# Routed experts in tiles of two 128-slot halves, each with its own expert

## The chip, the cores and the metric

The kernel runs on one NeuronCore of one Trainium2 chip. Five engines work side by side, each from its own instruction stream, and meet only at semaphores: TensorE (PE), VectorE (DVE), ScalarE (ACT), GpSimd (POOL) and SyncE (SP), whose queue issues most DMAs. The metric is the device time of one execution in microseconds. The kernel before takes 455.58 us, the median of three runs (455.02 to 456.61).

## The reference, cut to what matters

A block with gated cross attention and a gated mixture of experts, for 32 sequences of 128 tokens of width 128 (T = 4096 tokens):

```python
x = x + tanh(g_xattn[0]) * attention(layernorm(x), ctx)     # 16 heads of 8
xf = layernorm(x).reshape(4096, 128)
# two shared experts, of which the mean is taken
sh = gelu(einsum('td,sdh->sth', xf, sW1) + sb1)              # hidden 512
shared = (einsum('sth,shd->std', sh, sW2) + sb2).mean(axis=0)
# eight routed experts, two for each token
gates = xf @ rW + rb
topk_vals, topk_idx = top_k(gates, 2)
w = softmax(topk_vals) scattered to the chosen experts
h = gelu(einsum('td,edh->eth', xf, W1) + b1)
moe = einsum('te,etd->td', w, einsum('eth,ehd->etd', h, W2) + b2)
x = x + tanh(g_ffn[0]) * (shared + moe)
```

Each row of `xf` is normalised without a learnt scale, so its 128 values sum to zero.

## The kernel before, in words

The program runs in four stages that follow one another on one core.

**Attention** goes through 16 pairs of sequences, in turns (`turns`, t = 0 to 19) in which each engine does its share of several pairs at once. Queries and keys are split by POOL into two fp16 parts, written by SP to DRAM and read back in another layout. Beside this, the 40 half pieces of expert weights (`SPLITS`) are loaded into staging memory by SP (`load_weights`), measured, scaled and split into fp16 high and low parts by POOL (`split_weights`, from turn 6 on, as many in a turn as `SPLIT_IN` says). Every product with expert weights is then three fp16 matmuls: high times high, low times high, high times low.

**Shared experts** take 16 units (8 groups of 512 tokens by two experts). Beside them DVE picks two experts for each token, counts them, gives each choice a slot, and POOL scatters the normalised rows (with their destination index) into the DRAM list `xs`, sorted by expert. Each expert's slots are padded to a multiple of `TILE` = 256, so the list never holds more than `NTILE` = 39 tiles, and 39 are always run. `tilee` holds the expert of each tile.

**Routed experts** run tile by tile. For tile i: SP loads 256 rows (`XR`); PE transposes them (`row_transposes`, L1122), ACT copies the result (`routed_copy`, L820); PE multiplies with W1 in `routed_up` (L1132), four chunks of 128 hidden values by 256 slots; ACT applies bias and gelu chunk by chunk (`routed_gelu`, L828); DVE splits the result into fp16 high (L1561) and low (L1563) parts, two chunks at a time; PE multiplies with W2 in `routed_down` (L1144), 24 matmuls of 128 by 128; DVE scales and adds the second bias (L1571); POOL scatters two times 128 rows to the DRAM tensor `yd` (L650). PE's order within a step of the loop is up of tile i+1, transposes of tile i+3, down of tile i.

Which weights a tile multiplies with is known only at run time. `TileExperts.load` (L384) therefore reads `tilee` into registers of the engine's sequencer, `LOADS` = 3 tiles at a time, on PE, ACT and DVE, all within the last seven shared units. An address such as `bass.ds(e * HID + c * P, P)` is then worked out by register instructions in front of the matmul that uses it: a fused one for a chunk's first address, a plain one for each further address (FUSED_REGOPS and ALU_OP in the trace, ISA and REGISTER_ALU in the order of the program).

**The tail** reads `yd` back, weighs both choices of each token, adds them to the residual and stores the output.

The bias b1 reaches gelu as a per-partition column (`b1T`), picked by a register for routed tiles; the gates' bias rb is added by DVE.

## Time and profile before

| | |
|---|---|
| median of three runs | 455.58 us |
| the profiled execution | 454.94 us, span 453.1 us (1.8 us lie around the span) |
| mean granted TensorE clock | 0.977 of full speed |
| busy share of the span | PE 85%, DVE 85%, ACT 75%, POOL 68% |
| POOL time in the routed scatters (L650) | 86.8 us, 78 instructions |

Times within the kernel are microseconds from the start of the span. Attention lies at about 15 to 220 us, the shared experts reach to about 317 us, the routed experts to 432 us and the tail to 453 us. A stage's share of busy time tells little where several engines are near full; the chain of waits tells which of them ends last. Matmuls are pipelined on PE: a matmul of 128 columns is listed with 0.22 us, while the next one starts 0.06 us later, so the distance of starts is what counts. [...]

### The profile page before, as it was taken

The numbers are of one execution on the slowest core, as the hardware profiler recorded it, in microseconds if no ns is written. First come the engines' busy times: TensorE is split into PE (matmuls) and PEld (weight loads), VectorE is DVE, ScalarE is ACT, GpSimd is POOL, SyncE is SP. The second block draws the span as 40 slices with busy tenths as digits, with TensorE's granted clock in tenths as the row PEclk, the third lists the DMA queues.
The fourth block names the chain that finished last, engine by engine and source line by source line (L and its number), as shares of the span: only waits on it lengthen the run. The fifth ranks groups of instructions, "written<-read, shape, count | busy, mean of one in ns | idle before, by whom it ended". The sixth has DMA issues, their size and how long they took to land.

```text
span 453.1 us, 14622 instructions
## 1 busy us (share of the span) xinstructions
PE 386.3 (85%) x5155; PEld 316.6 (70%) x5155; DVE 384.9 (85%) x947; ACT 340.8 (75%) x677; POOL 309.7 (68%) x431
## 2 busy tenths in 40 slices
PE   0558889997999899988789999998999999999910
PEld 0335677786788788766557776777899999999900
DVE  7696668978876987899778999887799999999986
ACT  0635677787888788878789986775888888888844
POOL 6252222799899899978777767774177777777740
PEclk9999999999999999999899999999999999999975
DMA  7968884354333334474221111112223333355229
GB/s 192 314 196 214 206 186 110 90 138 98 92 92 98 87 95 107 101 229 175 92 66 49 55 37 53 49 48 69 70 83 96 97 90 93 94 156 158 69 78 294
DMA packets 71686, 53.43 MB, mean 118 GB/s; under 512 B 7209, under 2 KB 63476, under 8 KB 71616
## 3 DMA queue, kind: packets, MB, share of 16 engines
q1 hardware_dynamic: 64896, 43.15, 35.9%
q0 software_dynamic: 4544, 8.44, 5.6%
q10 hardware_dynamic: 2176, 0.91, 0.8%
q8 instruction: 44, 0.72, 0.7%
q14 instruction: 26, 0.21, 0.2%
HBM read 29.51 MB, written 24.33 MB: 119 GB/s over the span
## 4 chain that ended last, share of the span: by engine, by line
POOL 23%; PE 21%; DVE 20%; issue 13%; DMA 10%; SPq 6%; ACT 4%; POOLq 0%; DVEq 0%; ACTq 0%
POOL yd L650 9%; DVE HH L1533 5%; PE pAtt L1144 4%; DMA scr<-QKS 4%; PE pAtt L1090 2%; PE pS L1132 2%; PE pE L1132 2%; DVE t_MX L1257 2%; POOL t_STG L558 2%; POOL t_W2l L562 2%; POOL QKS L548 2%; PE pAtt L928 1%; DMA t_STG<-in_W 1%; POOL xs L628 1%; POOL t_XF L572 1%
## 5 line engine op out<-in xcount | busy, mean ns | idle before, releaser
L650 POOL DMA_INDIRECT yd<-Y,XR x78 | 86.8, 1113 | 37.6 <-issue 23.2
L1257 DVE TENSOR_REDUCE t_MX<-pS 128x4 f32<-128x512 f32 x128 | 86.8, 682 | 22.6 <-PE pS L889 20.0
L748 ACT ACTIVATE PT<-pE,t_mbias,t_scl 128x512 f32<-128x512 f32 x128 | 96.9, 789 | 2.7 <-PE pE L889 2.7
L628 POOL DMA_INDIRECT xs<-t_STG,t_pos x64 | 66.2, 1034 | 23.1 <-issue 14.3
L1563 DVE SCALAR_TENSOR_TENSOR HR<-GG,t_sc,HR 128x512 f16<-128x512 f32 x78 | 58.6, 751 | 2.8
L1144 PE MATMUL pAtt<-t_W2h,HR 128*128 x624 | 59.2, 219 | 0.7 <-DVE HR L1563 0.7
L889 PE MATMUL pS<-t_K,t_Q 128*128 128x128 f16 x512 | 52.0, 228 | 8.5 <-DVE t_MX L1257 5.1
L1144 PE MATMUL pAtt<-t_W2l,HR 128*128 x312 | 54.4, 219 | 0.0
L828 ACT ACTIVATE GG<-pS,t_b1T,t_inv 128x256 f32<-128x256 f32 x78 | 39.8, 561 | 16.9 <-PE pS L1132 16.9
L889 PE MATMUL pE<-t_Q,t_K 128*128 128x128 f16 x512 | 49.9, 220 | 1.6 <-DMA t_Q<-MPl 0.6
L1144 PEld LDWEIGHTS pAtt<-t_W2h,HR 128*128 128x128 f16 x624 | 49.6, 98 | 1.1 <-issue 0.9
L1090 PE MATMUL pAtt<-t_W2h,HH 128*128 128x128 f16 x512 | 46.4, 219 | 1.2 <-DVE HH L1533 1.0
L889 PEld LDWEIGHTS pS<-t_K,t_Q 128*128 128x128 f16 x512 | 35.1, 102 | 13.3 <-DVE t_MX L1257 8.0
L1090 PE MATMUL pAtt<-t_W2l,HH 128*128 128x128 f16 x256 | 44.0, 219 | 0.0
L1090 PEld LDWEIGHTS pAtt<-t_W2h,HH 128*128 128x128 f16 x512 | 40.1, 98 | 3.6 <-DVE HH L1533 2.0
L928 PE MATMUL pAtt<-PT,t_V 128*32 128x128 f32 x1024 | 42.0, 282 | 0.0
L889 PEld LDWEIGHTS pE<-t_Q,t_K 128*128 128x128 f16 x512 | 36.8, 98 | 6.9 <-ACT PT L748 3.8
L828 ACT ACTIVATE GG<-pE,t_b1T,t_inv 128x256 f32<-128x256 f32 x78 | 39.8, 567 | 0.0
L1561 DVE TENSOR_SCALAR HR<-GG,t_sc 128x512 f16<-128x512 f32 x78 | 37.8, 485 | 1.9 <-ACT GG L828 1.3
L546 POOL CAST QKS<-QK 128x512 f16<-128x512 f32 x16 | 9.8, 610 | 42.2 <-ACT QK L666 42.2
L1132 PE MATMUL pE<-XE,t_W1h 128*128 128x256 f16 x156 | 32.1, 273 | 0.0
L1132 PE MATMUL pS<-XE,t_W1h 128*128 128x256 f16 x156 | 31.9, 273 | 0.0
(280 smaller groups left out, 1042.7 us busy)
## 6 DMA issues: line engine op xcount, KB each, us to landing
xs<-t_padrow SPq DMA_DIRECT2D x10, 516.0 KB, 5.1
XR<-xs SPq DMA_DIRECT2D x39, 129.0 KB, 2.3
scr<-QKS SPq DMA_DIRECT2D x16, 256.0 KB, 2.4
t_Q<-scr SPq DMA_DIRECT2D x16, 256.0 KB
t_K<-scr SPq DMA_DIRECT2D x32, 128.0 KB
t_STG<-in_W SPq DMA_DIRECT2D x7, 512.0 KB, 6.6
YY<-yd SPq DMA_DIRECT2D x14, 256.0 KB, 4.2
t_X<-in_x SPq DMA_DIRECT2D x4, 512.0 KB, 7.7
```

What stands on the lines that cost most here:

```text
L628: g.indirect_dma_start(k.xs, bass.IndirectOffsetOnAxis(ap=pos[:, n:n + 1], axis=0), k.PAY[:, n, :], None).then_inc(h.di[q], 16)
L650: g.indirect_dma_start(k.yd, bass.IndirectOffsetOnAxis(ap=XR[u][:, q, D:ROW], axis=0), Y[u][:, q, :], None, bounds_check=2 * T - 1, oob_is ...
L748: act.activation(PT[:, m % NPT], pE[g % 2][:], ACT.Exp, bias=k.mbias[:, bt:bt + 1], scale=k.scl[:, bt:bt + 1]).then_inc(s.exp, 1)
L828: act.activation(G32[i % 2][:, c, :], pU[c][:, 0:TILE], ACT.Gelu, bias=k.b1T[:, bass.ds(e * NC + c, 1)], scale=k.inv[:, 3:4]).then_inc(r.g ...
L889: ins = pe.matmul(out[:, j, :], ko if transposed else qo, qo if transposed else ko, start=True, stop=True)
L928: ins = pe.matmul(pA[bb][32 * j:32 * j + 32, part // 2, :], k.V[pair % NB][:, 4 * bb + j, part, :], PT[:, m % NPT, j, :], start=(part == 0 ...
L1090: ins = pe.matmul(pA[u][:, q, :], HH[e][:, part, c, q * P:(q + 1) * P], w[:, w0:w0 + P], start=(e == 0 and c == 0 and q == 0 and step == 0 ...
L1132: ins = pe.matmul(pU[c][:, 0:TILE], w[:, bass.ds(e * HID + c * P, P)], XE[i % M][:, part, :], start=(step == 0), stop=(step == 2))
L1144: ins = pe.matmul(pA[i % 2][:, q, :], HR[i % M][:, part, c, q * P:(q + 1) * P], w[:, bass.ds(e * HID + c * P, P)], start=(c == 0 and q == ...
L1257: v.tensor_reduce(out=MX[:, n // G % 2, n % G // 4, m % 2, m // 2::2], in_=pS[n % 2][:], axis=AX_X, op=ALU.max).then_inc(s.max, 1)
L1561: v.tensor_scalar(HR[i % M][:, 0, ch, :], G32[i % 2][:, ch, :], k.sc[:, 2:3], None, ALU.mult).then_inc(r.hi, 1)
L1563: v.scalar_tensor_tensor(out=HR[i % M][:, 1, ch, :], in0=G32[i % 2][:, ch, :], scalar=k.sc[:, 2:3], in1=HR[i % M][:, 0, ch, :], op0=ALU.mu ...
```

## The change

`TILE` becomes 128, so 71 tiles (`NTILE`) are always run instead of 39. Two tiles form a duo of 256 slots, and the loop runs over 36 duos (the last has one half). Rows are loaded, transposed, activated and split for the duo as a whole. The products with weights are made for each half with that half's expert, so the up product has 24 matmuls of 128 slots instead of 12 of 256. The second bias is added for each half on its own.

The bias b1 becomes part of the product: as a row's values sum to zero, the last weight row can be subtracted from the other 127 (`fold_last_row` on POOL, with the last row broadcast to all partitions by `load_last_rows` on SP), the last value of each row is set to 1, and the last weight row is replaced by b1 (`hidden_biases`). The same is done for rb in the gates. Gelu then needs no bias column, and takes two chunks (128 by 512) at once; the high part of the second two chunks is made by ACT (`routed_rounding`) instead of DVE. All W1 pieces are now split ahead of all W2 pieces; the W2 pieces are loaded into the place of the broadcast rows, after the fold. `LOADS` becomes 2, and what the shared units don't load is loaded in the routed loop, one load in a step, on PE and DVE; ACT needs none.

```diff
-TILE = 256
+TILE = 128
 NTILE = (2 * T + E * (TILE - 1)) // TILE
-SLOTS = NTILE * TILE
+DUO = 2 * TILE
+NDUO = -(-NTILE // 2)
+SLOTS = NDUO * DUO
...
-    LOADS = 3
+    LOADS = 2
...
+    FOLDS = {LAG: (0, 1), LAG + 1: (2, 3), LAG + 2: (4,)}
...
+            def load_last_rows(n):
+
+                w = (io.W1, io.sW1)[2 * n >= E]
+                e = 2 * n % E
+                for j in range(2):
+                    sp.dma_start(k.weight_pieces[PIECES + n][:, j * HID:(j + 1) * HID], w[e + j, LASTC, :].partition_broadcast(P)).then_inc(k.s_row[n // 3], 16)
+
+            def hidden_biases():
+
+                sp.wait_ge(s.fold, PIECES)
+                sp.dma_start(k.STG[LASTC:D, 0:E * HID], io.b1.rearrange("(o e) h -> o (e h)", o=1)).then_inc(k.s_b1, 16)
+                sp.dma_start(k.STG[LASTC:D, E * HID:NE * HID], io.sb1.rearrange("(o e) h -> o (e h)", o=1)).then_inc(k.s_b1, 16)
...
-                for n in {1: range(4, 6), 2: range(6, 8), 3: range(8, 10)}.get(t, ()):
-                    load_weights(n)
+                if t == 1:
+                    load_weights(PIECES - 1)
+                for n in {1: (0,), 2: (1, 2), 3: (3, 4)}.get(t, ()):
+                    load_last_rows(n)
+                if t == LAG + 2:
+                    hidden_biases()
+                for n in {LAG + 1: (0, 1), LAG + 2: (2, 3), LAG + 3: (4,)}.get(t, ()):
+                    sp.wait_ge(s.fold, n + 1)
+                    load_weights(PIECES + n)
...
+            def fold_last_row(n):
+
+                if n == 0:
+                    g.wait_ge(s.sq, PIECES)
+                g.wait_ge(k.s_row[n // 3], 16 * 2 * (3, 2)[n // 3])
+                for j in range(2):
+                    piece = k.weight_pieces[n][:, j * HID:(j + 1) * HID]
+                    ins = g.tensor_tensor(piece, piece, k.weight_pieces[PIECES + n][:, j * HID:(j + 1) * HID], ALU.subtract)
+                ins.then_inc(s.fold, 1)
...
+                    g.wait_ge(k.s_b1, 32)
                     tables()
+                for n in FOLDS.get(t, ()):
+                    fold_last_row(n)
...
-            for i in range(NTILE):
+            for i in range(NDUO):
                 u = i % N
                 g.wait_ge(r.y, i + 1)
-                for q in range(2):
+                for q in range(parts_of(i)):
...
-            def routed_gelu(i, e, c):
-                act.wait_ge(r.up, NC * i + c + 1)
-                if c % 2 == 0:
-                    wait(act, r.lo, NC // 2 * (i - 2) + c // 2 + 1)
-                act.activation(G32[i % 2][:, c, :], pU[c][:, 0:TILE], ACT.Gelu, bias=k.b1T[:, bass.ds(e * NC + c, 1)], scale=k.inv[:, 3:4]).then_inc(r.gelu, 1)
+            def routed_gelu(i, half):
+                ch, wide = slice(2 * half, 2 * half + 2), TILE * parts_of(i)
+                act.wait_ge(r.up, 2 * i + half + 1)
+                wait(act, r.lo, 2 * (i - 2) + half + 1)
+                act.activation(G32[i % 2][:, ch, 0:wide], pair_of_chunks(i, half)[:, :, 0:wide], ACT.Gelu, scale=k.inv[:, 3:4]).then_inc(r.gelu, 1)
+
+            def routed_rounding(i):
+                wide = TILE * parts_of(i)
+                act.wait_ge(r.gelu, 2 * i + 2)
+                wait(act, r.dn, i - M + 1)
+                act.activation(HR[i % M][:, 0, 2:4, 0:wide], G32[i % 2][:, 2:4, 0:wide], ACT.Copy, scale=k.sc[:, 2:3]).then_inc(r.hia, 1)
...
                 for c in range(NC):
-                    wait(pe, r.gelu, NC * (i - 1) + c + 1)
-                    for step, (w, part) in enumerate(((k.W1h, 0), (k.W1l, 0), (k.W1h, 1))):
-                        ins = pe.matmul(pU[c][:, 0:TILE], w[:, bass.ds(e * HID + c * P, P)], XE[i % M][:, part, :], start=(step == 0), stop=(step == 2))
-                    ins.then_inc(r.up, 1)
+                    if c % 2 == 0:
+                        wait(pe, r.gelu, 2 * (i - 2) + c // 2 + 1)
+                    out = pair_of_chunks(i, c // 2)[:, c % 2, :]
+                    for q in range(last + 1):
+                        tok = slice(q * TILE, (q + 1) * TILE)
+                        for step, (w, part) in enumerate(((k.W1h, 0), (k.W1l, 0), (k.W1h, 1))):
+                            ins = pe.matmul(out[:, tok], w[:, bass.ds(es[2 * i + q] * HID + c * P, P)], XE[i % M][:, part, tok],
+                                            start=(c % 2 == 0 and q == 0 and step == 0), stop=(c % 2 == 1 and q == last and step == 2),
+                                            skip_group_check=True)
+                    if c % 2:
+                        ins.then_inc(r.up, 1)
...
-                    for q in range(2):
+                    for q in range(parts_of(i)):
                         for step, (w, part) in enumerate(((k.W2h, 0), (k.W2l, 0), (k.W2h, 1))):
-                            ins = pe.matmul(pA[i % 2][:, q, :], HR[i % M][:, part, c, q * P:(q + 1) * P], w[:, bass.ds(e * HID + c * P, P)],
+                            ins = pe.matmul(pA[i % 2][:, q, :], HR[i % M][:, part, c, q * P:(q + 1) * P], w[:, bass.ds(es[2 * i + q] * HID + c * P, P)],
...
-            for i in range(NTILE):
-                if i + 1 < NTILE:
-                    routed_up(i + 1, es[i + 1])
-                if i + 3 < NTILE:
+            for i in range(NDUO):
+                if i + 1 < NDUO:
+                    routed_up(i + 1)
+                tile_experts.load()
+                if i + 3 < NDUO:
                     row_transposes(i + 3)
-                routed_down(i, es[i])
+                routed_down(i)
...
             def routed_split(i):
+                wide = TILE * parts_of(i)
                 for half in range(2):
                     ch = slice(2 * half, 2 * half + 2)
-                    v.wait_ge(r.gelu, NC * i + 2 * half + 2)
-                    wait(v, r.dn, i - M + 1)
...
+                    if half == 0:
+                        v.wait_ge(r.gelu, 2 * i + 1)
+                        wait(v, r.dn, i - M + 1)
...
+                    else:
+                        v.wait_ge(r.hia, i + 1)
...
-                v.scalar_tensor_tensor(out=Y[u][:], in0=pA[i % 2][:, 0:2, :], scalar=k.down[:, 0:1], in1=row.to_broadcast([P, 2, D]),
-                                       op0=ALU.mult, op1=ALU.add).then_inc(r.y, 1)
+                for q in range(parts_of(i)):
+                    ins = v.scalar_tensor_tensor(out=Y[u][:, q, :], in0=pA[i % 2][:, q, :], scalar=k.down[:, 0:1], in1=k.b2[:, bass.ds(es[2 * i + q] * D, D)],
+                                                 op0=ALU.mult, op1=ALU.add)
+                ins.then_inc(r.y, 1)
```

How this stands in the order of the program, at three places. First PE, one chunk of the up product of a routed tile before (L1132: W1h and W1l are the weights' high and low parts, XE the transposed rows, pE the chunk's PSUM bank; ISA and REGISTER_ALU are the register instructions that work out an address):

```order
L1132 ISA [waits x_gelu]
L1132 MATMUL pE<-XE,t_W1h 128x256
L1132 REGISTER_ALU
L1132 MATMUL pE<-XE,t_W1l 128x256
L1132 MATMUL pE<-XE,t_W1h 128x256
```

and one chunk of a duo now (L1186):

```order
L1186 ISA [waits x_gelu]
L1186 MATMUL pE<-XE,t_W1h 128x128
L1186 REGISTER_ALU
L1186 MATMUL pE<-XE,t_W1l 128x128
L1186 MATMUL pE<-XE,t_W1h 128x128
L1186 ISA
L1186 MATMUL pE<-XE,t_W1h 128x128
L1186 REGISTER_ALU
L1186 MATMUL pE<-XE,t_W1l 128x128
L1186 MATMUL pE<-XE,t_W1h 128x128
```

Each 256-wide group of three matmuls with one pair of register instructions has become two 128-wide groups with a pair each.

Second PE, from the end of an up product over the transposes (pMix) into the down product (pAtt), before (L1144):

```order
L1132 MATMUL pE<-XE,t_W1h 128x256
L1122 MATMUL pMix<-t_ident,XR 128x128 [waits x_XE,x_ld4]
L1122 MATMUL pMix<-t_ident,XR 128x128 x3
L1144 REGISTER_ALU [waits x_lo,x_y]
L1144 MATMUL pAtt<-t_W2h,HR 128x128
L1144 REGISTER_ALU
L1144 MATMUL pAtt<-t_W2l,HR 128x128
L1144 MATMUL pAtt<-t_W2h,HR 128x128 x2
L1144 MATMUL pAtt<-t_W2l,HR 128x128
L1144 MATMUL pAtt<-t_W2h,HR 128x128
```

and now (L1201):

```order
L1186 MATMUL pE<-XE,t_W1h 128x128
L394 TENSOR_LOAD tilee
L1171 MATMUL pMix<-t_ident,XR 128x128 [waits x_XE,x_ld3]
L1171 MATMUL pMix<-t_ident,XR 128x128 x3
L1201 REGISTER_ALU [waits x_lo,x_y]
L1201 MATMUL pAtt<-t_W2h,HR 128x128
L1201 REGISTER_ALU
L1201 MATMUL pAtt<-t_W2l,HR 128x128
L1201 MATMUL pAtt<-t_W2h,HR 128x128
L1201 REGISTER_ALU
L1201 MATMUL pAtt<-t_W2h,HR 128x128
L1201 REGISTER_ALU
```

The load of two expert numbers (TENSOR_LOAD, in 22 of the 36 steps) stands between up and transposes, and the down product has two register instructions for every three matmuls where it had two for every six.

Third SP's queue at the end of turn 4 and the start of turn 5 (t_K is the keys' place in SBUF, t_rows the bounds on the weights, scr the DRAM copy of queries and keys), before:

```order
L487 DMA t_Q<-scr 64x8x256
L490 DMA t_K<-scr 32x8x256 x2
L435 DMA t_rows<-kwm 128x384
L467 DMA scr<-QKS 128x2x512
L469 DMA scr<-QKS 128x2x256
```

and now:

```order
L514 DMA t_Q<-scr 64x8x256
L517 DMA t_K<-scr 32x8x256 x2
L439 DMA t_STG<-in_W 128x8x128 x2
L462 DMA t_rows<-kwm 128x384
L494 DMA scr<-QKS 128x2x512
L496 DMA scr<-QKS 128x2x256
```

Two weight loads that stood at the ends of turns 1 and 2 are now issued here, ahead of the load of the bounds and of the next turn's stores.

## Rows read from the trace of the kernel before

**Rows 1.** View by stretch: length, busy of PE, PEld, DVE, ACT, POOL, clock, DMA

```profile
320.00:432.00 112.00, 111.34 (x1540) 104.90 (x1537) 107.53 (x194) 94.00 (x194) 82.87 (x74) 1.00 0.33 96
```

**Rows 2.** Chain of waits, two routed tiles: start us, length us, what ended last

```profile
331.01 1.34 PE pAtt L1144 x24
332.35 0.66 PE pS L1132 x6
333.01 0.66 PE pE L1132 x6
...
333.89 1.34 PE pAtt L1144 x24
```

**Rows 3.** Groups of instructions, 320 to 432 us: count | busy us, mean ns

```profile
L1561 DVE TENSOR_SCALAR HR<-GG,t_sc 128x512 f16<-128x512 f32 x78 | 37.8, 485 | 1.9 <-ACT GG L828 1.3
...
L1563 DVE SCALAR_TENSOR_TENSOR HR<-GG,t_sc,HR 128x512 f16<-128x512 f32 x78 | 58.6, 751 | 2.8
...
L1571 DVE SCALAR_TENSOR_TENSOR Y<-pAtt,t_down,t_b 128x256 f32<-128x256 f32 x38 | 18.1, 478 | 0.0
...
L828 ACT ACTIVATE GG<-pE,t_b1T,t_inv 128x256 f32<-128x256 f32 x78 | 39.8, 567 | 0.0
...
L820 ACT ACTIVATE XE<-pMix 128x512 f16<-128x512 f16 x37 | 22.5, 608 | 0.0
```

**Rows 4.** The same view, ACT in the shared experts, 225 to 317 us

```profile
L795 ACT ACTIVATE HH<-GG,t_sc 128x512 f16<-128x512 f32 x22 | 15.7, 730 | 0.0
...
L803 ACT ACTIVATE GG<-pS,t_b1T,t_inv 128x512 f32<-128x512 f32 x16 | 11.6, 781 | 5.4 <-PE pS L1027 5.4
```

**Rows 5.** Instructions of L1132, 345.6 to 346.6 us; PEldq is PE's sequencer

```profile
L1132 PEldq FUSED_REGOPS  x4: 46/46/46, 345.7 to 346.4; - x4
L1132 PEldq ALU_OP  x4: 32/32/32, 345.8 to 346.5; - x4
...
L1132 PE MATMUL pS<-XE,t_W1h x1: 273/273/273, 346.6 to 346.6; 128*128 128x256 f16 x1
```

**Rows 6.** The same view of L1144, 346.9 to 348.4 us

```profile
L1144 PEldq ALU_OP  x8: 32/32/32, 347.0 to 348.3; - x8
```

**Rows 7.** Instructions of PE in order of time, first routed tile

```profile
320.82 0.28 PE L1132 MATMUL pE<-XE,t_W1h 128*128 128x256 f16 x1
320.94 0.27 PE L1132 MATMUL pE<-XE,t_W1l 128*128 128x256 f16 x1
...
321.99 0.22 PE L1144 MATMUL pAtt<-t_W2h,HR 128*128 x1
322.10 0.22 PE L1144 MATMUL pAtt<-t_W2l,HR 128*128 x1
```

**Rows 8.** Instructions that read tilee: duration min/median/max ns, first and last start

```profile
L384 PEldq TENSOR_LOAD <-tilee x13: 762/794/963, 281.8 to 314.4; - x13
```

**Rows 9.** Instructions of POOL in order of time, turn 4

```profile
59.03 0.61 POOL L546 CAST QKS<-QK 128x512 f16<-128x512 f32 x1 [5.60 <-ACT QK L666]
59.72 1.16 POOL L548 TENSOR_TENSOR QKS<-QK,QKS 128x512 f16<-128x512 f32 x1
```

**Rows 10.** Instructions of SP's queue in order of time, end of turn 4

```profile
70.50 0.45 SPq L435 DMA_DIRECT2D t_rows<-kwm  x1
72.25 0.38 SPq L467 DMA_DIRECT2D scr<-QKS  x1
```

**Rows 11.** Chain of waits, after the last tile

```profile
434.88 0.87 POOL yd L650
...
436.17 3.12 DMA yd<-Y,XR
```

**Rows 12.** View by stretch, around the one dip of the clock in mid-kernel

```profile
219.00:220.00 1.00, 0.08 (x1) 0.11 (x1) 0.93 (x4) 0.00 (x0) 0.92 (x2) 1.00 0.07 19
221.00:222.00 1.00, 0.98 (x10) 0.55 (x12) 0.90 (x5) 1.00 (x4) 0.85 (x3) 0.50 0.00 0
```

**Rows 13.** Groups of instructions of PE inside that dip, 221 to 224 us

```profile
L889 PE MATMUL pE<-t_Q,t_K 128*128 128x128 f16 x4 | 0.6, 308 | 0.0
```

More of the change, by code:

```diff
@@ L241, in layer @@
     SPLIT = LAG + 3
-    FIRST_W2 = 12
-    SPLITS = [(which, e, half) for which, e in ((0, 8), (0, 9), (0, 0), (0, 4), (0, 1), (0, 5), (1, 0), (1, 1), (1, 2), (1, 3), (0, 2), (0, 6), (1, 4),
-                                                (0, 3), (0, 7), (1, 5), (1, 8), (1, 9), (1, 6), (1, 7)) for half in range(2)]
+    FIRST_W2 = 2 * NE
+    SPLITS = [(which, e, half) for which, e in ((0, 8), (0, 9), (0, 0), (0, 4), (0, 1), (0, 5), (0, 2), (0, 6), (0, 3), (0, 7),
+                                                (1, 0), (1, 1), (1, 2), (1, 3), (1, 4), (1, 5), (1, 8), (1, 9), (1, 6), (1, 7)) for half in range(2)]
     UNITS = len(SPLITS)
@@ L280, in layer @@
     XR = [lt(f"XR{u}", [P, 2, ROW], I32) for u in range(N)]
-    XE = [lt(f"XE{u}", [P, 2, TILE], F16) for u in range(M)]
-    GG = lt("GG", [P, 2, NC, TILE])
+    XE = [lt(f"XE{u}", [P, 2, DUO], F16) for u in range(M)]
+    GG = lt("GG", [P, 2, NC, DUO])
     G32 = [GG[:, u] for u in range(2)]
     HS = [GG[:].rearrange("p u c t -> p (u c t)").rearrange("p (c t) -> p c t", c=NC), H32[:]]
-    HR = [lt(f"HR{u}", [P, 2, NC, TILE], F16) for u in range(M)]
+    HR = [lt(f"HR{u}", [P, 2, NC, DUO], F16) for u in range(M)]
     Y = [lt(f"Y{u}", [P, 2, D]) for u in range(N)]
@@ L367, in load_results, with parts_of @@
         eng.dma_start(YY[:, j, R * n:R * n + R, :], yv[:, j, R * n:R * n + R, :]).then_inc(f.ld[j][n], 16)
+    def parts_of(i):
+        return min(2, NTILE - 2 * i)
     def all_scattered(eng):
         for u in range(N):
-            eng.wait_ge(r.st[u], 32 * len(range(u, NTILE, N)))
+            eng.wait_ge(r.st[u], 16 * sum(parts_of(i) for i in range(u, NDUO, N)))
     class TileExperts:
@@ L801, in shared_body @@
                     wait(act, h.lo, NC * (i - 2) + c + 1)
-                    col = (E + i % 2) * NC + c
-                    act.activation(HS[i % 2][:, c, :], pU[c], ACT.Gelu, bias=k.b1T[:, col:col + 1], scale=k.inv[:, 3:4]).then_inc(h.gelu, 1)
+                    act.activation(HS[i % 2][:, c, :], pU[c], ACT.Gelu, scale=k.inv[:, 3:4]).then_inc(h.gelu, 1)
                     if c - 1 in on_scalar(i):
                         rounding(i, c - 1)
-                    if c % 2 and i >= LOADING:
-                        tile_experts.load()
                     if i == 3 and c == 0:
@@ L876, in _ @@
             pe.transpose(pA[0][:, 1, 0:B], k.maskf[:], k.identf[0:B, 0:B]).then_inc(s.mr, 1)
-            pe.wait_ge(s.md, 1)
+            pe.wait_ge(s.mb, 2)
             pe.matmul(pA[1][:, 0, 0:5], k.ones[0:5, :], k.mxd[:], start=True, stop=True)
-            pe.matmul(pA[1][:, 1, 0:B], k.ones[:], k.maskT[:], start=True, stop=True).then_inc(s.ma, 1)
+            pe.matmul(pA[1][:, 1, 0:B], k.ones[:], k.maskT[:], start=True, stop=True).then_inc(s.mr, 1)
             pe.wait_ge(k.s_rest, k.rest_in)
-            pe.transpose(b1_cols, k.b1r[:], k.identf[0:NE * NC, 0:NE * NC])
             pe.wait_ge(s.bvr, 1)
@@ L1152, in _ @@
             row_transposes(1)
-            routed_up(0, es[0])
+            routed_up(0)
             row_transposes(2)
-            for i in range(NTILE):
-                if i + 1 < NTILE:
-                    routed_up(i + 1, es[i + 1])
-                if i + 3 < NTILE:
+            for i in range(NDUO):
+                if i + 1 < NDUO:
+                    routed_up(i + 1)
+                tile_experts.load()
+                if i + 3 < NDUO:
                     row_transposes(i + 3)
-                routed_down(i, es[i])
+                routed_down(i)
         @block.vector
@@ L1569, in routed_result @@
                 wait(v, r.st[u], 32 * (i // N))
-                row = k.b2[:, bass.ds(e * D, D)].rearrange("p (o d) -> p o d", o=1)
-                v.scalar_tensor_tensor(out=Y[u][:], in0=pA[i % 2][:, 0:2, :], scalar=k.down[:, 0:1], in1=row.to_broadcast([P, 2, D]),
-                                       op0=ALU.mult, op1=ALU.add).then_inc(r.y, 1)
+                for q in range(parts_of(i)):
+                    ins = v.scalar_tensor_tensor(out=Y[u][:, q, :], in0=pA[i % 2][:, q, :], scalar=k.down[:, 0:1], in1=k.b2[:, bass.ds(es[2 * i + q] * D, D)],
+                                                 op0=ALU.mult, op1=ALU.add)
+                ins.then_inc(r.y, 1)
             es = tile_experts.of
             routed_split(0)
-            for i in range(NTILE):
-                if i + 1 < NTILE:
+            for i in range(NDUO):
+                if i + 1 < NDUO:
                     routed_split(i + 1)
-                routed_result(i, es[i])
+                tile_experts.load()
+                routed_result(i)
             weights_of_choices()
@@ L1625, in program @@
         k.s_c, k.s_x = ([outer.enter_context(nc.semaphore(f"{n}{c}")) for c in range(NT // CHUNK)] for n in ("c_ctx", "c_x"))
-        k.s_one, k.s_pad, k.s_padk, k.s_b2, k.s_rest = (outer.enter_context(nc.semaphore("c_" + n)) for n in ("one", "pad", "padk", "b2", "rest"))
+        k.s_one, k.s_pad, k.s_padk, k.s_b2, k.s_rest, k.s_b1 = (outer.enter_context(nc.semaphore("c_" + n)) for n in ("one", "pad", "padk", "b2", "rest", "b1"))
+        k.s_row = [outer.enter_context(nc.semaphore(f"w_row{n}")) for n in range(2)]
         k.keep = outer
```

88 lines of the change are left out of this document (48 added, 40 removed).

## The prediction

> **What bounds the kernel now.** I read the view by stretch first, to see which stage the change touches and who is full there. In the routed stage, 320 to 432 us, PE is busy 111.34 of 112 us and DVE 107.53, at full clock [rows 1]: two engines are nearly level, so neither can be named from shares. The chain of waits decides: it runs on PE alone, tile after tile, with 1.34 us for the 24 matmuls of a down product, twice 0.66 us for an up product, and 2.88 us from one down product to the next [rows 2]; what is left, 2.88 - 1.34 - 1.32 = 0.22 us, are the four transposes. 39 tiles by 2.88 are the 112 us. DVE, by the groups of instructions, has twice 0.485 and 0.751 and once 0.478 us, 2.95 us with overlaps in it [rows 3], so it comes close behind.
>
> The third view is the one that matters here: the instructions that PE's sequencer handles itself. While the array is in the middle of the down product, the sequencer already works on the next tile's up product: its four fused and four plain register instructions lie between 345.7 and 346.5 us, and the first matmul that uses them starts at 346.6 [rows 5]. So the sequencer runs ahead, and its register work costs nothing now. How fast it can go is in the same rows: eight register instructions, with twelve matmuls between them, from 345.7 to 346.5, are seven distances of 0.114 us. One such instruction lasts 0.032 or 0.046 us, but the next is not begun for 0.11 to 0.12 us, however many matmuls stand between. Eight of a down product go from 347.0 to 348.3 [rows 6], a wait for DVE among them. A tile has 16 of them, 16 x 0.115 = 1.84 us, and 0.5 us lie between the last of the up product (346.5) and the first of the down product (347.0), 0.4 us more than the usual distance, for waits and transposes: 2.2 us of sequencer in a tile of 2.88 us. It has 0.6 us to spare.
>
> What happens when it is not ahead can be seen at the first routed tile, where the array had waited: the first two matmuls of the down product start 0.11 us apart (321.99 and 322.10), and those of an up chunk 0.12 us (320.82 and 320.94) [rows 7], where 1.34 / 24 = 0.056 us is the array's own distance. Each waits for its register instruction.
>
> **The change part by part.**
>
> *Array work.* The up product has 24 matmuls of 128 columns for 12 of 256. By the down product's 0.056 us [rows 2] that is 1.34 us for 1.32: nothing. A duo would still take the array 2.9 us, and 36 duos with a half last one, 35.5 x 2.88 = 102 us for 112. That would be the gain.
>
> *Register work.* A chunk's pair of register instructions is now needed for each half, and the down product has two for every three matmuls instead of every six: 8 fused and 24 plain ones in a duo, 32 for 16. At 0.115 us each that is 3.68 us, with 0.4 us for waits 4.08 us. This is more than the array's 2.9 us, so the sequencer can no longer be ahead, and every distance is its own. 35.5 x 3.68 + 36 x 0.4 = 130.6 + 14.4 = 145.0 us. The stretch that I measure from begins behind the first up product, 16 x 0.115 = 1.8 us, so 143.2 us.
>
> *Loads of expert numbers.* 22 of the 36 steps now hold one on PE, between up and transposes. Before, all 13 were in the shared stage, 0.762 to 0.963 us each, median 0.794 [rows 8], for three numbers. For two numbers there is no row; from below it could be two thirds of the shortest, 0.51, from above 0.96. I take the median, as the row nearest to it, and one distance behind it: 0.9 us. With no lead left, nothing hides it: 22 x 0.9 = 19.8 us. Queued behind it on PE are the transposes and the down product. A 14th load now stands ahead of the first routed product: +0.9 us. DVE has its loads too, but its own work is 0.49 + 2 x 0.75 + two results of at most 0.48 each [rows 3] and 0.9, under 3.9 us, inside PE's step. ACT has two gelus at 0.78, a rounding at 0.73 [rows 4] and a copy at 0.61 [rows 3], 2.9 us. Neither ends last, and the half of the high part that moves from DVE to ACT, a good thing where DVE was level with PE, is worth nothing.
>
> So the stretch takes 143.2 + 19.8 = 163 us instead of 112: +51 us.
>
> *Tail.* The last duo has one scatter less behind it; in the chain, two scatters start 1.29 us apart (434.88 and 436.17) [rows 11]: -1.3 us.
>
> *Attention.* The fold adds ten POOL operations of 128 x 512. The nearest row is the subtraction of queries' and keys' high parts, 1.16 us [rows 9]: 11.6 us in turns 3 to 5, four in turns 3 and 4 each, 4.6 us. POOL idles 5.60 us ahead of turn 4's first operation [rows 9], waiting for ACT, so this is covered; without the cover it would be +11.6 us on POOL at most. SP issues ten broadcast loads and two bias loads more, and five weight loads later. At the end of turn 4 SP is free from 70.95 to 72.25 us [rows 10], room for the two weight issues of 0.45 us that now stand there. The bytes of turns 1 to 3 stay nearly the same (2.5 MB of rows for the 2.5 MB of W2), and 2.5 MB more move in turns 4 to 6, beside the transfers that the chain there waits for; no row prices that. From below it is nothing, or a little gain, as the measuring of the fifth piece no longer waits for the sixth; from above I put what the fold would cost uncovered, 11.6 us, for fold and transfers together. I take 0, since POOL's cover and SP's gap are rows, and keep -1 and +11.6.
>
> *Sum.* 454.94 + 51 + 0.9 - 1.3 = 505.5 us against the profiled execution; that lies 0.6 us under the median of the runs shown, so about 506; I say 505.
>
> [...]
>
> **The rivals.**
>
> *A. The register work stays hidden, loads too: faster.* Then the stage is 102 us, and the time 454.94 - 10 - 1.3 = 443.6, 444 us. For it: PE shows no gap today with 16 register instructions in a tile. Against it: [rows 5 and 7]. It decides if 32 of them and 0.4 us fit into 2.88 us, at 0.077 us or less each; no row shows a distance under 0.11. Chance 0.05.
>
> *B. Register work hidden, the 22 loads exposed.* 444 + 20.7 = 464 us. It needs the same distance and fails by the same rows. Chance 0.03.
>
> *C. The clock falls.* [...] It did so once in mid-kernel, after a second in which PE was busy 0.08 us of 1.00; there four matmuls of 128 columns, each 0.308 us long, took 0.6 us [rows 12, 13], so (0.6 - 0.308) / 3 = 0.10 us apart. The 52 matmuls of a duo would then take the array 5.2 us, over the sequencer's 4.1 to 5.0: 35.5 x 5.2 = 185 us, 22 more, 527 us. Against it: a duo still gives the array 2.9 us of work in 4.1 to 5.0, far from the 0.08 of 1.00. Chance 0.07. [...]
>
> *D. Attention pays for fold and transfers:* +11.6 us, 517 us. For it are the ten operations and 2.5 MB in later turns, against it the idle time in [rows 9, 10]. Chance 0.04.
>
> **How the numbers follow.** The forecast has 0.80, with its own range from 0.105 us and 0.6 us a load (-11.4 and -6.6: 487) to 0.12 us and 1.0 us (+5.7 and +2.2: 513). Slower by over 0.3% (what a measurement of this kernel can tell from no change) are the forecast, B, C and D, 0.94; faster is A, 0.05; for a sum of gains and costs that happens to land within 0.3% I leave 0.01. The range takes in the bounds of the distance, the load and D, and C's 527: 487 to 528.
>
> **What would show it.** In the changed kernel's routed stage: starts of the first two matmuls of each down triple 0.11 us apart and of each up triple 0.12; 8 fused and 24 plain register instructions in a step of some 4.1 us, 4.9 with a load; DVE, ACT and POOL idle and waiting for PE; matmuls following their register instruction by 0.1 us instead of 0.9. The forecast is wrong if a down product still takes 1.34 us (A), if the steps with and without a load are alike, or if the clock reads under 1.00 there (C).

## The result, and the profile after

| | kernel before | kernel after |
|---|---|---|
| time, median | 455.69 us (4 runs) | 509.88 us (4 runs) |
| profiled execution | 454.94 us | 510.11 us, span 508.4 us |
| busy share of PE, DVE, ACT, POOL in the routed stage | 99%, 96%, 84%, 74% | 94%, 56%, 56%, 44% |
| a step of the routed loop, mean | 2.86 us a tile, 39 tiles | 4.53 us a duo, 35.5 duos |

The kernel after is slower: 1.114 times the time before, 95% interval 1.104 to 1.125. The ratio is that of the fast runs, so it leaves out one slow run of 513.23 us, which the median holds. The forecast was 505 us, in a range of 487 to 528.

The view by stretch of the kernel after, from the first routed work to the last product (length; busy time of PE, PEld, DVE, ACT, POOL; granted clock, DMA share, GB/s; PEld are PE's weight loads, LDWEIGHTS in the trace, 0.096 us each at L1201):

```profile
320.00:487.00 167.00, 156.48 (x1889) 131.90 (x1885) 93.67 (x181) 93.78 (x146) 73.34 (x68) 1.00 0.24 68
```

It answers to [rows 1]. The window holds 167 us where that one held 112 (its first 2.5 us are still shared experts here); DVE fell from 96% of it to 56%, and the clock stayed at 1.00, where the stretch from 221 to 222 us of before reads 0.50 [rows 12]. PE still reads 94% busy, and this is the trap of this trace: a matmul is listed with about 0.22 us from start to end, so matmuls that start 0.11 us apart overlap in the records, and the engine counts as busy though it does less than two thirds of the work that it could: as shown further down, the array alone would need 2.84 of the 4.53 us of a step. Starts have to be read, not shares. The instructions of PE in order of time (start us, length us) show it, first in an up product and then from the transposes into a down product:

```profile
339.83 0.22 PE L1186 MATMUL pS<-XE,t_W1l 128*128 128x128 f16 x1
...
340.12 0.22 PE L1186 MATMUL pS<-XE,t_W1l 128*128 128x128 f16 x1
340.17 0.30 PE L1186 MATMUL pS<-XE,t_W1h 128*128 128x128 f16 x2
```

```profile
341.83 0.22 PE L1201 MATMUL pAtt<-t_W2h,HR 128*128 x1
341.94 0.22 PE L1201 MATMUL pAtt<-t_W2l,HR 128*128 x1
342.00 0.27 PE L1201 MATMUL pAtt<-t_W2h,HR 128*128 x2
```

From 341.83 to 341.94 it is 0.11 us, as at the one place of before where PE had caught up with its sequencer [rows 7]; the third of the triple, which needs no new address, follows after 0.06. An up triple takes 0.29 us, from 339.83 to 340.12, where three of the array's own distances of 0.056 us are 0.17.

The chain of waits in the loop answers to [rows 2]. Two duos with a load of expert numbers (the loads go on to the 22nd step), and one later without:

```profile
339.00 2.09 PE pS L1186 x24
341.10 0.51 issue
341.61 0.38 PE pMix L1171 x4
342.00 1.93 PE pAtt L1201 x24
343.92 2.05 PE pE L1186 x24
345.97 0.45 issue
346.43 0.38 PE pMix L1171 x4
346.81 1.98 PE pAtt L1201 x24
```

```profile
459.60 0.28 PE pAtt L1201 x4
459.87 0.03 issue
459.90 1.69 PE pAtt L1201 x20
461.59 2.08 PE pS L1186 x24
463.68 0.24 PE pMix L1171 x4
463.92 1.91 PE pAtt L1201 x24
```

In these lines the down product takes 1.91 to 2.00 us for 1.34, the up product 2.05 to 2.09 for 1.32. From one down product to the next it is 4.81 us with a load (342.00 to 346.81) and 4.32 without (459.60 to 463.92). The load is in no line of PE: it is the piece called issue between up product and transposes, 0.45 to 0.51 us.

The instructions listed under PEldq, PE's sequencer, of one up product and one down product, and the loads, of which the window holds 20 (duration ns min/median/max, first and last start us):

```profile
L1186 PEldq FUSED_REGOPS  x8: 46/46/46, 338.9 to 340.6; - x8
L1186 PEldq ALU_OP  x8: 32/32/32, 339.0 to 340.7; - x8
```

```profile
L1201 PEldq ALU_OP  x16: 32/32/32, 341.7 to 343.6; - x16
```

```profile
L394 PEldq TENSOR_LOAD <-tilee x20: 533/537/541, 326.3 to 419.1; - x20
```

Against [rows 5, 6] two things changed. There are twice as many register instructions, 8 fused with 8 plain ones in the up product and 16 in the down product, which has plain ones alone. And they stand beside the matmuls that use them: the up product's lie between 338.9 and 340.7, inside the product itself (339.00 to 341.10), where before they lay wholly in the product ahead. The load of two numbers takes 0.537 us, where three took 0.794 [rows 8].

What DVE and ACT wait for says the same. Their groups between 320 and 487 us (count, busy us, mean ns of one, idle us before them and what ended it):

```profile
L1626 DVE SCALAR_TENSOR_TENSOR HR<-GG,t_sc,HR 128x512 f16<-128x512 f32 (+1 forms) x72 | 53.6, 745 | 18.1 <-ACT HR L877 16.7
L1622 DVE TENSOR_SCALAR HR<-GG,t_sc 128x512 f16<-128x512 f32 (+1 forms) x36 | 17.4, 482 | 38.3 <-ACT GG L871 38.3
```

```profile
L871 ACT ACTIVATE GG<-pS,t_inv 128x512 f32<-128x512 f32 x36 | 24.7, 687 | 35.2 <-PE pS L1186 35.2
L871 ACT ACTIVATE GG<-pE,t_inv 128x512 f32<-128x512 f32 (+1 forms) x36 | 24.2, 675 | 34.2 <-PE pE L1186 34.1
```

ACT's two groups now wait 69 us for up products, and DVE's two 55 us for ACT. Before, DVE's two waited 1.3 us for ACT [rows 3], and of ACT's two the one in [rows 3] waited 0 us and the other 16.9:

```profile
L828 ACT ACTIVATE GG<-pS,t_b1T,t_inv 128x256 f32<-128x256 f32 x77 | 39.4, 561 | 16.9 <-PE pS L1132 16.9
```

### The profile page after: what moved, and what is told of

Same layout as the page of the kernel before. It is cut to its first block, busy times and chain, and to the rows that moved or that the text cites. A ratio compares the mean times of both kernels' runs of the same rounds, so it can differ in the third digit from the quotient of the medians.

```text
span 508.4 us, 15533 instructions
## 1 busy us (share of the span) xinstructions
PE 426.3 (84%) x5442; PEld 339.0 (67%) x5442; DVE 370.8 (73%) x932; ACT 333.2 (66%) x626; POOL 311.8 (61%) x435
## 4 chain that ended last, share of the span: by engine, by line
PE 58%; DVE 18%; DMA 8%; issue 5%; ACT 3%; POOL 2%; SPq 2%; DVEq 0%; ACTq 0%; POOLq 0%
PE pAtt L1201 13%; PE pS L1186 7%; PE pE L1186 7%; PE pAtt L1139 5%; PE pAtt L977 4%; DMA scr<-QKS 4%; DVE HH L1592 3%; PE pS L1076 3%; PE pE L1076 2%; PE pE L938 2%; PE pS L938 2%; PE pMix L1171 2%; DVE t_MX L1317 2%; PE pMix L919 2%; DMA t_STG<-in_W 1%
## 5 line engine op out<-in xcount | busy, mean ns | idle before, releaser
L698 POOL DMA_INDIRECT yd<-Y,XR x71 | 76.4, 1075 | 97.6 <-DVE Y L1634 86.7
L1317 DVE TENSOR_REDUCE t_MX<-pS 128x4 f32<-128x512 f32 x128 | 86.5, 681 | 21.3 <-PE pS L938 19.2
L1201 PE MATMUL pAtt<-t_W2h,HR 128*128 x568 | 72.8, 217 | 0.0
L1626 DVE SCALAR_TENSOR_TENSOR HR<-GG,t_sc,HR 128x512 f16<-128x512 f32 (+1 forms) x72 | 53.6, 745 | 18.1 <-ACT HR L877 16.7
L1201 PE MATMUL pAtt<-t_W2l,HR 128*128 x284 | 61.4, 216 | 0.1
L1201 PEld LDWEIGHTS pAtt<-t_W2h,HR 128*128 128x128 f16 x568 | 51.1, 96 | 2.5
L871 ACT ACTIVATE GG<-pS,t_inv 128x512 f32<-128x512 f32 x36 | 24.7, 687 | 35.2 <-PE pS L1186 35.2
L871 ACT ACTIVATE GG<-pE,t_inv 128x512 f32<-128x512 f32 (+1 forms) x36 | 24.2, 675 | 34.2 <-PE pE L1186 34.1
L1622 DVE TENSOR_SCALAR HR<-GG,t_sc 128x512 f16<-128x512 f32 (+1 forms) x36 | 17.4, 482 | 38.3 <-ACT GG L871 38.3
L1186 PE MATMUL pS<-XE,t_W1h 128*128 128x128 f16 x288 | 38.0, 222 | 0.2
L1186 PE MATMUL pE<-XE,t_W1h 128*128 128x128 f16 x280 | 37.6, 222 | 0.1
L1634 DVE SCALAR_TENSOR_TENSOR Y<-pAtt,t_down,t_b 128x128 f32<-128x128 f32 x71 | 21.7, 346 | 15.4 <-PE pAtt L1201 14.7
```

Source lines behind the costliest of these rows:

```text
L698: g.indirect_dma_start(k.yd, bass.IndirectOffsetOnAxis(ap=XR[u][:, q, D:ROW], axis=0), Y[u][:, q, :], None, bounds_check=2 * T - 1, oob_is ...
L871: act.activation(G32[i % 2][:, ch, 0:wide], pair_of_chunks(i, half)[:, :, 0:wide], ACT.Gelu, scale=k.inv[:, 3:4]).then_inc(r.gelu, 1)
L1186: ins = pe.matmul(out[:, tok], w[:, bass.ds(es[2 * i + q] * HID + c * P, P)], XE[i % M][:, part, tok], start=(c % 2 == 0 and q == 0 and st ...
L1201: ins = pe.matmul(pA[i % 2][:, q, :], HR[i % M][:, part, c, q * P:(q + 1) * P], w[:, bass.ds(es[2 * i + q] * HID + c * P, P)], start=(c == ...
L1317: v.tensor_reduce(out=MX[:, n // G % 2, n % G // 4, m % 2, m // 2::2], in_=pS[n % 2][:], axis=AX_X, op=ALU.max).then_inc(s.max, 1)
L1626: v.scalar_tensor_tensor(out=HR[i % M][:, 1, ch, 0:wide], in0=G32[i % 2][:, ch, 0:wide], scalar=k.sc[:, 2:3], in1=HR[i % M][:, 0, ch, 0:wide],
```

## The experiments

The theory: the routed loop goes at the pace at which TensorE's sequencer works off register instructions, 32 in a duo, and each load of expert numbers comes on top. Rival 1: weights and moving operands of 128 columns are slow by themselves. Rival 2: the loads inside the loop are the main loss. Rival 3: the gelu of two chunks and the other orders on VectorE and ScalarE hold the products. One row of each kernel is enough to compare the loops: the 568 (before: 624) matmuls with the high part of W2 run from the first down product to the last. For the kernels before and after:

```profile
L1144 PE MATMUL pAtt<-t_W2h,HR x624: 216/219/219, 322.0 to 431.8; 128*128 x156
```

```profile
L1201 PE MATMUL pAtt<-t_W2h,HR x568: 216/217/219, 327.3 to 486.8; 128*128 x190
```

So 109.8 us before, 159.5 after. The stretch of which prediction and expectations speak begins 2.0 to 2.8 us earlier, with the second up product: 111.8 and 162.3 us. A kernel's time without an interval is that of a single run. In all kernels of this section the granted clock is 1.00 in the loop (340 to 400 us).

**One expert for both halves.** It halves the register instructions and changes nothing else on the engines' side.

```diff
- w[:, bass.ds(es[2 * i + q] * HID + c * P, P)]      # up and down
+ w[:, bass.ds(es[2 * i] * HID + c * P, P)]
```

> Both halves of a duo take TensorE's weights of the first half's expert, so half of the outputs of mixed duos leave out their own expert; the matmuls, their shapes, the loads of the experts' numbers and all of VectorE's and ScalarE's work stay. A duo then has 16 register instructions on TensorE's sequencer and not 32. Theory (the sequencer's register instructions set the step of a duo): 4 fused x 0.124 + 12 plain x 0.112 = 1.84 us, with about 0.6 us of waits 2.4 us, and 3.0 us with a load of 0.6 us in it; the array wants about 2.9 us, so a duo takes 2.9 to 3.05 us, the stretch of the routed loop 104 to 110 us where it is 162 us now, the whole 452 to 458 us. Rival 1 (weights and moving operands of 128 columns are slower by themselves): no change, about 510 us. Rival 2 (the loads inside the loop stop the array whatever stands around them): 36 x 2.9 + 22 x 0.6 = 118 us for the stretch, 466 us or more. Rival 3 (the gelu of two chunks and the other orders on VectorE and ScalarE hold the products): no change, about 510 us.

Measured: 452.46 us.

```profile
L1201 PE MATMUL pAtt<-t_W2h,HR x568: 216/219/219, 327.2 to 429.4; 128*128 x190
```

The loop takes 102.2 us, 57 less, with the same 22 loads and the same 128-column matmuls, and with VectorE and ScalarE as they were. Rivals 1 and 3 are out. Rival 2 is out as well: the loop holds 21 of the 22 loads, which exposed would be 11 us at 0.537 us each, and it is 2 us longer than the one without any load that follows.

**Experts fixed in the program.**

```diff
- w[:, bass.ds(es[2 * i + q] * HID + c * P, P)]      # up and down, no load on TensorE
+ w[:, slice((2 * i + q) % E * HID + c * P, (2 * i + q) % E * HID + c * P + P)]
```

> TensorE's experts are numbers written into the program (half n of the slots takes expert n mod 8), so the products leave out the routing; no register instruction and no load of a number is left on TensorE's sequencer, while matmuls, shapes and the other engines' work stay. Theory (register instructions and loads together are the whole loss): a duo takes what the array wants, 2.85 to 2.95 us, the stretch 103 to 106 us, the whole 448 to 455 us. Rival 1 (128-column matmuls are slower): about 510 us. Rival 3 (VectorE's and ScalarE's order): about 510 us. If it comes out well below the kernel with one expert for both halves, the difference is the loads' part.

Measured: 447.1 us.

```profile
L1201 PE MATMUL pAtt<-t_W2h,HR x568: 216/219/220, 324.2 to 424.4; 128*128 128x128 f16 x190
```

100.2 us: this is the array's own time for the changed loop. 35 steps and a last half product (0.67 us, half of [rows 2]'s 1.34) make (100.2 - 0.7) / 35 = 2.84 us a step. Register instructions and loads together cost 59.3 us of the 159.5.

**Register instructions added to the kernel before.** The other direction: matmuls of 256 columns, tiles with one expert, all as before, and only eight more register instructions in the down product.

```diff
+ twin.append((es[i + 1] + es[0]).with_bounds(min_val=0, max_val=E - 1))   # es[0] is 0
- w[:, bass.ds(e * HID + c * P, P)]                  # down
+ w[:, bass.ds((e2 if q else e) * HID + c * P, P)]   # e2 = twin[i]
```

> The kernel before, with nothing left out and the same matmuls in tiles of 256 slots; only the addresses of the second half's rows in the down product are worked out from a second copy of the expert's number (the number plus the first tile's, which is 0), so that 8 more register instructions a tile stand on TensorE's sequencer: 24 where it has 16. Theory (16 are hidden under the array's 2.88 us, more are not): 8 fused x 0.124 + 16 plain x 0.112 = 2.78 us, with 0.4 to 0.6 us of waits 3.2 to 3.4 us a tile, 0.3 to 0.5 us over 2.88 in each of 39 tiles: 467 to 475 us. Rival 1 (it is the 128-column shapes): no change, 455 us, since the shapes here are those of before. A rival by a queue ahead of the array that is deep enough: 455 us.

Measured: 472.47 us, 17 more than before. The chain of waits of one tile, and the extent of the loop:

```profile
344.31 0.78 PE pS L1132 x6
345.09 0.66 PE pE L1132 x6
345.75 0.22 PE pMix L1122 x4
345.97 1.64 PE pAtt L1144 x24
347.61 0.78 PE pS L1132 x6
```

```profile
L1144 PE MATMUL pAtt<-t_W2h,HR x624: 215/219/228, 322.4 to 448.8; 128*128 x156
```

The step is 3.30 us (344.31 to 347.61) where it was 2.88, and most of it is the down product, now with 16 instructions, which went from 1.34 to 1.64 us. The same matmuls thus become slower by register instructions alone, and the point from which they cost lies between 16 and 24 a tile.

**No loads inside the loop.** The register instructions stay at 32 a duo.

```diff
- tile_experts.load()                                # in the loop
+ es = [loaded[n] if n < len(loaded) else (loaded[n % len(loaded)] + loaded[n // len(loaded) - 1]).with_bounds(...) ...]
```

> The kernel after, without TensorE's 22 loads inside the routed loop: the halves from the 29th on take the experts of the first 28 (so the outputs leave out their own expert), by an expression that keeps the number of register instructions at 32 a duo. Theory (with 32 register instructions the sequencer sets the step, so each load adds what it takes, 0.54 us and its distance to the next, 0.6 us): the stretch falls by 22 x 0.6 = 13 us, from 162 to 149 us, all duos take about 4.27 us as the ones without a load do now, the whole 495 to 499 us. Rival (the loads are hidden, the step is held by something else): the stretch stays at 162 us. Rival 2 of the first runs (the loads are the main loss): the stretch falls to about 110 us.

Measured: 494.64 us.

```profile
347.25 2.05 PE pE L1186 x24
349.30 0.24 PE pMix L1171 x4
349.54 2.00 PE pAtt L1201 x24
```

```profile
L1201 PE MATMUL pAtt<-t_W2h,HR x568: 216/217/219, 323.9 to 471.5; 128*128 x190
```

The loop takes 147.6 us, 11.9 less than after. The first of the 22 loads stands ahead of the first down product, so this is 0.57 us for each of 21: the load's own 0.537 us and little more. So with 32 register instructions in a duo, where the sequencer sets the step, a load costs all of itself, and with one expert for both halves, where it does not, the same loads cost at most 2 us in all (102.2 us for 100.2).

**Addresses worked out together.** The four addresses of a chunk are worked out ahead of its six matmuls, next to each other, so that the compiler packs them into fused instructions: 12 in a duo where 32 instructions stood.

```diff
+ def addresses(i, c, ws, stationary):
+     for q in range(parts_of(i)):
+         for w in ws:
+             pe.lower_ap(w[:, bass.ds(es[2 * i + q] * HID + c * P, P)], for_matmul_weights=stationary)
...
+ addresses(i, c, (k.W1h, k.W1l), True)     # up, ahead of a chunk's matmuls
+ addresses(i, c, (k.W2h, k.W2l), False)    # down
```

> The kernel after, with nothing left out; the addresses are worked out together in the up product alone (8 fused instructions where 16 stood), the down product keeps its 16 plain ones. Theory: 4 x 0.15 + 4 x 0.115 + 16 x 0.112 = 2.85 us, with 0.5 us of waits 3.35 us, with a load 3.95 us: 22 x 3.95 + 13.5 x 3.35 = 132 us for the stretch (162 after, 100 with both products fused), the whole 476 to 484 us. If the array's 2.83 us hid everything up to its own length in each product, 448 us; if only the down product mattered (its matmuls follow addresses one by one), about 500 us.

> The kernel after, with nothing left out; only the four addresses that a chunk needs (two halves by the two pieces of the weights) are worked out together ahead of the chunk's six matmuls, so that they go into fused register instructions: 12 a duo (4 of six operations, 4 of two, 4 of four) where it has 32 now. Theory: a fused one of three operations took 0.124 us against 0.112 us for a plain one, so 12 take about 12 x 0.14 = 1.7 us, with 0.5 us of waits 2.2, with a load 2.8: under the array's 2.9 us, a duo takes 2.9 to 3.0 us, the stretch 104 to 109 us, the whole 452 to 458 us. If the time of a fused instruction goes with its operations instead (0.112 us each), nothing changes: about 505 us. Rivals 1 and 3 (128 columns, the other engines' order): about 510 us. Rival 2 (loads): 466 us or more.

Measured with the up product alone changed: 477.07 us; with both: 447.99 us, median of 5, 0.9825 of before with an interval of 0.978 to 0.987, and 4 us under the range expected. The extents, first with up alone:

```profile
L1207 PE MATMUL pAtt<-t_W2h,HR x568: 216/217/220, 325.0 to 454.2; 128*128 x190
```

```profile
L1208 PE MATMUL pAtt<-t_W2h,HR x568: 219/219/229, 327.6 to 427.9; 128*128 x190
```

129.2 and 100.3 us. The second is the 100.2 us of the program without any register instruction or load: all of the 59 us came back, the loads with them. The sequencer is ahead again: the matmuls of a down product start 0.06 us apart, also behind a new address (345.05 and 345.11). In the view by stretch PE has no gap (60.00 of 60.00 us), DVE is at 91%, and eight fused instructions lie between 345.5 and 346.5 us while the down product of the duo before is still under way:

```profile
340.00:400.00 60.00, 60.00 (x1079) 60.00 (x1077) 54.58 (x104) 52.91 (x83) 44.95 (x42) 1.00 0.35 97
```

```profile
345.05 0.22 PE L1208 MATMUL pAtt<-t_W2h,HR 128*128 x1
345.11 0.22 PE L1208 MATMUL pAtt<-t_W2l,HR 128*128 x1
```

```profile
L1177 PEldq FUSED_REGOPS  x8: 42/58/79, 345.5 to 346.5; - x8
```

From 325 to 427 us PE's sequencer has 415 FUSED_REGOPS and no ALU_OP here, 12 fused ones a duo. In this version the addresses are both packed and moved ahead of the matmuls, and moving them alone was not tried. My estimate is that it would not have been enough: 32 plain instructions at the 0.112 us of the kernel after are 3.6 us, more than the array's 2.84.

**The kernel before with its addresses worked out together** (the same helper, two addresses a chunk).

> The kernel before, with nothing left out and only the addresses worked out together: 8 fused register instructions a tile of 256 slots where it has 16 register instructions. Theory (16 were hidden under the array's 2.88 us): the stretch of the routed loop stays at 110 us or loses up to 1 us, the whole 454 to 455.5 us; the 7 us by which the kernel after with fused addresses is ahead of before then come from 35.5 duos where 39 tiles stood (3.5 x 2.83 = 10 us, less what the earlier stages lost). Rival (the register instructions held the array in before, too): 39 x 8 x 0.112 = up to 35 us less, or any part of it over 2 us.

Measured: 454.33 us, median of 10, ratio 0.998 (0.996 to 1.000).

```profile
L1150 PE MATMUL pAtt<-t_W2h,HR x624: 219/219/230, 320.8 to 430.4; 128*128 x156
```

109.6 us for 109.8: where the 16 instructions of a tile are hidden, taking half of them away brings nothing that can be told from nothing. So what the version above wins over before comes from 35.5 steps for 39, 9.5 us in the loop.

**The stall at the start.** In its profiled execution the kernel after comes 4 us late to the first routed matmul (322.52 us for 318.51), and all of it is there from the first split of query and key weights on: 23.89 us before, 27.83 after. Transfers issued by ScalarE, listed under ACTq (start, length of the issue), before and after:

```profile
9.57 0.69 ACTq L165 DMA_DIRECT2D t_rb<-in_rb  x1
11.27 0.34 ACTq L167 DMA_DIRECT2D kmd<-t_kmrow  x1
```

```profile
9.85 5.02 ACTq L168 DMA_DIRECT2D t_rWf<-in_rb  x1
14.91 0.32 ACTq L170 DMA_DIRECT2D kmd<-t_kmrow  x1
```

The router's bias used to be broadcast to 128 partitions and is now one row into partition 127; its issue takes 5.02 us for 0.69. At the end of this block the other engines wait for ScalarE: its last instruction there ends at 17.08 us, and the next ones come from 17.50 us on, on SyncE at 17.50, on ScalarE at 17.52 and on VectorE at 17.55 after 5.65 us idle. Three places for that one row were tried: SyncE (one line moved from ScalarE's list of transfers to behind SyncE's last load of x), SyncE together with the router's weights, and ScalarE's seventh place; the last two with addresses worked out together.

> The kernel after, with nothing left out; only the transfer of the one row of the router's bias into partition 127 is issued by SyncE behind its last load of x and no more by ScalarE. In the trace its issue held ScalarE for 5.02 us, and every engine waits for ScalarE at the end of that block; the first split of the query and key weights then came at 27.83 us where it came at 23.89 before. Theory A (that one row's issue is the stall): ScalarE ends the block about 4 us earlier, the first split comes at 23.5 to 24.5 us, the whole is 3 to 5 us less (about 505.5 us). Theory B (ScalarE's queue of transfers is full, and whatever stands at that place waits): the next issue (key mask or the broadcast row) takes the stall, the first split stays at 27 to 28 us, the whole within 1 us of 510. Theory C: the stall moves to SyncE and ends as late there; no change.

> The kernel with fused addresses in both products (448 us), with both transfers into the router's weights issued by SyncE behind its last load of x and no more by ScalarE; nothing is left out. With one of them moved, the first split of the query and key weights came at 25.95 us, where 26.4 to 28.0 stood in the kernels without the move and 23.89 in the kernel before. Theory B (ScalarE's queue of transfers is backed up, so fewer transfers on it shorten it): key mask issued at 11.3 us with 0.3 to 1 us, ScalarE ends the block near 13.5 us, the first split at 23.5 to 24.5 us, the whole 2 to 3 us less, 445 to 446 us. If the stall stays with the key mask's transfer (2 us, as with one moved), the split comes at 25.5 to 26 us and the whole within 1 us of 447.5.

> The kernel with fused addresses in both products, where the one-row transfer of the router's bias is ScalarE's seventh and not its fifteenth; nothing is left out. The one row's issue took 5.02, 5.39, 3.20 and 3.12 us as the fifteenth on ScalarE, 1.12 us on SyncE from 10.51 us and 3.66 us on SyncE from 13.91 us. Theory (a transfer of one row waits at its issue while the loads of x and the context are under way, wherever it stands behind them): issued at 4 us, ahead of the backlog, it takes about 0.5 us, ScalarE ends its block at 13.5 to 14 us, the first split of the query and key weights comes at 23.9 to 24.5 us (26.4 with the row fifteenth), the whole is 2 to 3 us less than 448: 445 to 446 us. Rival (ScalarE's queue takes so many transfers and the fifteenth stalls whatever it is): the stall stays with the next transfer, the split at 26 to 28 us, the whole at 448 us.

Measured: 508.36 us (1.118 of before, 1.111 to 1.126), 450.43 us (0.988, 0.984 to 0.993) and 448.16 us (0.985, 0.982 to 0.988); first splits at 25.95, 28.39 and 25.89 us. The issues in question, of the second and of the third of these kernels:

```profile
8.93 4.41 SPq L136 DMA_DIRECT2D t_X<-in_x  x1
...
13.91 3.66 SPq L138 DMA_DIRECT2D t_rWf<-in_rb  x1
```

```profile
4.01 0.54 ACTq L165 DMA_DIRECT2D t_rWf<-in_rb  x1
...
11.29 2.01 ACTq L171 DMA_DIRECT2D kmd<-t_kmrow  x1
```

Issued at 4.01 us the row takes 0.54 us, so it is not slow in itself; as ScalarE's fifteenth transfer, issued at 9.70 to 10.90 us, it took 3.12 to 5.39 us in six kernels, and on SyncE 3.66 us at 13.91 us and 1.12 at 10.51. But with the row at 4.01 us the key mask's transfer, with as many transfers ahead of it as in the kernel before, takes 2.01 us for 0.34. None of the times expected for the second and the third came out, and the second's first split came later than in any other of these kernels. Neither theory holds alone: the stall is partly the row's and partly moves to its neighbour. Why the key mask did not wait in the kernel before stays open, and issuing the row after this block was not tried. For the whole time the three moves decide little: the third is level with the version without a move (448.16 and 447.99).

## Why the prediction was right

The order and the size came out by the mechanism named: 510.11 us in the profiled execution, 55.2 more than the profiled 454.94, where the sum had 50.6. Of the 55.3 us between the two spans, 50.5 lie in the stretch behind the first up product (162.3 us for 111.8), 4.5 ahead of it and 0.3 in the tail.

- *The bound before, and 16 hidden instructions.* Right: adding eight makes the step longer, halving them changes nothing.
- *Array work, "35.5 x 2.88 = 102 us for 112".* Right: with the sequencer free the loop takes 100.2 us and the stretch 102.5.
- *Register work, 4.08 us a duo.* Right in kind, 0.1 to 0.2 us short: 4.32 in the chain, (147.6 - 0.95) / 35 = 4.19 on average without loads. The distances were right (0.11 us in a down triple); the term that was too small is the 0.4 us for waits and transposes. With the median distances of this trace, 0.124 us behind a fused and 0.112 behind a plain instruction, 8 and 24 make 3.68 us, so 0.5 us is left for it. The tile with 24 leaves the same: 3.28 on average less 8 x 0.124 + 16 x 0.112 = 2.78 is 0.50.
- *Loads, 0.9 us each, 19.8 us.* Too much: without them the stretch is 149.9 us, so they cost 12.4, 0.56 us each. Two numbers take 0.537 us; I took the median of the loads of three, and most of the distance behind it that I added was already in the step. The two misses, 149.9 us where the sum had 143.2 and 12.4 where it had 19.8, cancel by luck, so the stretch of 163 us (measured 162.3) looks better than its terms.
- *The 14th load, +0.9.* Nothing of it can be seen: the first routed matmul is 4.0 us late, as the first split already was.
- *Tail, -1.3.* Wrong by 1.6 us: from the last down matmul to the end it is 21.6 us for 21.3. I took the chain's scatters [rows 11] as what a duo less would shorten; after, the chain goes from the last product to the weights of the choices on DVE (1.2 us, 487.50 to 488.72) and on to the final sums, and the scatters are not in it. They did come sooner, the last one 3.3 us behind the last matmul's start (490.13) where it was 4.3 (436.17).
- *Attention, 0.* The fold was hidden as said: from the first to the last split it is 160.3 us for 160.0. What came is 4 us at a place that I had not priced, ScalarE's issue of one row. I had looked at POOL and SP for moved work, and not at the transfers that ScalarE issues in the first block, though the diff puts two there.
- *Rival A and B* fell with the distances. *Rival C* fell too: 1.00 throughout the routed stage. The dip cited there came behind one idle of PE of 2.07 us, up to 219.92 us, of which [rows 12] show one microsecond (where the prediction says a second), and the clock read 0.89 from 220 to 221 us and 0.50 from 221 to 224. The idles here are shorter: 21 steps between 326 and 426 us hold one of 0.45 to 0.61 us each, and the clock read 1.00 all the while. *Rival D* had the right sign and the wrong place.

Rival A's 444 us did not come about with 32 register instructions: with their waits they take the sequencer 4.19 us in a step for which the array needs 2.84. With 12 fused ones they and the loads stay hidden: the loop takes 100.3 us for 100.2 without any.

## What to carry to other kernels

An address that depends on a run-time number cost TensorE's sequencer 0.112 to 0.124 us an instruction here. 16 of them in a tile of 2.88 us were hidden (the loop took 109.8 us with 16 and 109.6 with 8), 24 made the step 3.30 us, and 32 made it 4.32 without a load, where the array needs 2.84. Cutting the tile by expert, with the matmuls of the up product halved in columns, took them from 16 to 32, so count them before such a cut. Work the addresses of several matmuls out next to each other, so that they are packed, 32 into 12: here that turned 1.114 into 0.983 of the time before, with the smaller tiles kept. And read the starts of matmuls, not PE's busy share, which still read 94% while the array had 1.6 times the time it needed.

## What was not expected of the hardware

- With the addresses worked out together the fused register instructions last 42, 55 to 60, or 74 to 79 ns (42 and 79 are the ends of the row of L1177 above), which I take for those of two, four and six operations, against 32 ns for a plain one; twelve of them did the work of 32, in a loop of 100.3 us for 100.2 without any.
- The issue of a one-row transfer took 5.02 us at 9.85 us and 0.54 us at 4.01 us, where the broadcast of the same row to 128 partitions took 0.69 us at 9.57 us.
- A load of two numbers into TensorE's registers took 0.537 us, and cost all of that where the sequencer set the step (0.57 us each) and next to nothing where the array did (at most 2 us for 21).
